# Pairing the key halves for the attention maxima: one 1024-column reduction, and seven PSUM banks shared out anew

## The reference

```python
xs = jnp.reshape(x, (B, T, C))                       # B 16, T 1024, C 128, x is layer-normed
scores = jnp.einsum('bhtd,bhsd->bhts', q, k) * scale # q, k: 8 heads x 1024 x 16
att = jax.nn.softmax(scores, axis=-1)                # needs the maximum over all 1024 keys
out = jnp.einsum('bhts,bhsd->bhtd', att, v)
...
x = x + _L0_conv_ref(_ln_c(x), ...)
t = _to_tokens(x)
t = t + _L0_ffn_ref(_ln_t(t), w_gating, w1, w2)      # top-2 gating over 16 experts
```

## Time and profile before

| | us |
|---|---|
| median of 3 runs | 2329.85 |
| lowest, highest | 2327.37, 2330.93 |
| span of the profiled execution | 2326.0 |
| TensorE busy (records overlap the drain) | 2117.5 (91%) |
| VectorE busy | 1840.5 (79%) |
| ScalarE busy | 1544.5 (66%) |

### The profile page before, as it was taken

One profiled execution on the slowest core, in us unless ns is written; L12 is line 12 of the kernel. 1 busy time (PEld: TensorE's weight loads), 2 busy tenths in 40 slices (PEclk: granted clock), 3 DMA queues, 4 the chain that ended last, 5 costly groups with the idle time before them and its releaser, 6 DMA issues. The chain is left out here.

```text
span 2326.0 us, 48689 instructions
## 1 busy us (share of the span) xinstructions
PE 2117.5 (91%) x14610; PEld 1160.1 (50%) x14610; DVE 1840.5 (79%) x4370; ACT 1544.5 (66%) x3153; POOL 1046.1 (45%) x1650
## 2 busy tenths in 40 slices
PE   6989999998999999999989999999888999999996
PEld 3333333333333333333333333333328999999996
DVE  6899989899899989899898999999954544445564
ACT  1677777777776777767676767777664666556553
POOL 3203444443434444444534445444344577645442
PEclk9999999999999999999999999999998999999997
DMA  4222223231323233231323332232233222222576
GB/s 123 47 41 57 57 56 69 42 71 35 68 47 65 49 67 61 49 74 35 68 39 64 55 63 58 56 59 43 61 118 112 72 71 82 89 65 70 155 241 184
DMA packets 135676, 170.79 MB, mean 73 GB/s; under 512 B 31568, under 2 KB 101592, under 8 KB 135414
## 3 DMA queue, kind: packets, MB, share of 16 engines
q1 hardware_dynamic: 118582, 134.25, 26.7%
q0 software_dynamic: 16896, 34.12, 4.2%
HBM read 64.86 MB, written 48.87 MB: 49 GB/s over the span
## 5 line engine op out<-in xcount | busy, mean ns | idle before, releaser
L978 DVE TENSOR_REDUCE sb_m_red<-banks 128x1 f32<-128x512 f32 x2048 | 1326.4, 678 | 154.6 <-PE banks L1491 153.1
L818 ACT ACTIVATE sb_arena_a<-banks 128x512 f32<-128x512 f32 x2048 | 1114.7, 599 | 444.3 <-PE banks L1515 421.2
L1491 PE MATMUL banks<-sb_arena_b 62*128 62x512 f32 x2048 | 815.2, 468 | 104.6 <-DVE sb_m_red L978 91.8
L1515 PE MATMUL banks<-sb_arena_b 64*128 64x512 f32 x2048 | 807.6, 463 | 7.1 <-ACT sb_arena_a L818 7.0
L1491 PEld LDWEIGHTS banks<-sb_arena_b 62*128 62x128 f32 x2048 | 347.6, 188 | 770.7 <-DVE sb_m_red L978 658.1
L1532 PE MATMUL banks<-sb_arena_a,sb_arena_d 128*32 128x512 f32 x4096 | 552.2, 611 | 6.5 <-ACT sb_arena_a L818 0.7
L747 POOL DMA_INDIRECT sorted_rows<-sb_rows,sb_place x256 | 251.4, 982 | 349.0 <-PE banks L1515 318.1
L791 POOL DMA_INDIRECT expert_out<-sb_arena_d x272 | 272.0, 1000 | 240.1 <-DVE sb_arena_d L1368 178.1
L1515 PEld LDWEIGHTS banks<-sb_arena_b 64*128 64x128 f32 x2048 | 338.4, 186 | 28.4 <-ACT sb_arena_a L818 28.0
L1657 PE MATMUL banks<-sb_arena_d,sb_arena_c 128*128 128x128 f32 x2176 | 290.8, 277 | 0.5 <-DVE sb_arena_c L1358 0.5
L1666 PE MATMUL banks<-sb_arena_c 128*128 128x128 f32 x2176 | 288.3, 276 | 0.0
(11 more groups left out here) (166 smaller groups left out, 1620.1 us busy)
## 6 DMA issues: line engine op xcount, KB each, us to landing
sb_arena_b<-sb_arena_c SPq DMA_DIRECT2D x768, 64.0 KB, 2.3
sb_arena_d<-sorted_rows SPq DMA_DIRECT2D x272, 66.0 KB
sb_x_in<-in_x_dram SPq DMA_DIRECT2D x16, 512.0 KB, 3.5
sb_res<-in_x_dram SPq DMA_DIRECT2D x16, 512.0 KB, 3.2
sb_x_all<-sb_res SPq DMA_DIRECT2D x16, 512.0 KB, 3.1
expert_out<-sb_arena_d POOLq DMA_INDIRECT x272
sorted_rows<-sb_rows,sb_place POOLq DMA_INDIRECT x256
sb_arena_a<-in_L_ffn_w_dram SPq DMA_DIRECT2D x4, 1024.0 KB, 7.1
```

Source lines behind the costliest of these rows:

```text
L818: nc.scalar.activation(probs[:, u % PRING, :], ps_score[:, u % RING, :], ACT.Exp, scale=SCALE).then_inc(exp_done, 1)
L978: nc.vector.tensor_reduce(out=m_red[:, s % 2, at:at + 1], in_=ps_max[:, m % SLOTS % RING, :], axis=AX.X, op=ALU.max).then_inc(max_taken, 1)
L1491: nc.tensor.matmul(ps_max[:, m % SLOTS % RING, :], qs[rows_of, g, l, half * HALF + t * P:half * HALF + (t + 1) * P], ks[rows_of, g, l, kh ...
L1515: nc.tensor.matmul(ps_score[:, u % RING, :], ks[rows_of, g, l, i * P:(i + 1) * P], qs[rows_of, g, l, half * HALF:(half + 1) * HALF], start ...
```

## The change

The two key halves of the same 128 queries and head now stand in neighbouring units: unit m even is keys 0 to 511, m odd keys 512 to 1023, and `side` changes every two units. They go to neighbouring banks of a ring of four (banks 3 to 6), and VectorE takes both with one maximum of 1024 columns, negated, straight into `m_neg`; `row_maxima` and `m_red` are gone. `LEAD` is 44, the order of a step's four heads is 1, 3, 0, 2 (`HEAD_AT`), so that M and S keep to opposite rows. The two steps of `split_m` come one step earlier. `ps_pv` is bank 7. There is no `misc` bank: scores and all other products go round the banks 0 to 2 in the order in which TensorE issues them (`front_order`), each waiting for the reader of the product three before it. `choose` starts at step 36 instead of 38.

```diff
-LEAD = 45
+LEAD = 44
+HEAD_AT = (1, 3, 0, 2)
 MSLOT = 24
-RING = 3
+FRONT, MRING = 3, 4
...
+FRONT_BANK = {what: n % FRONT for n, what in enumerate(front_order())}
...
-        ps_score, ps_max = banks[:, 0:RING], banks[:, RING:2 * RING]
-        ps_pv, misc = banks[:, 6], banks[:, 7]
+        ps_max, ps_pv = banks[:, FRONT:FRONT + MRING], banks[:, FRONT + MRING]
+        def front(what, b, i=0):
+            return banks[:, 4] if b == B - 1 and what in LATE else banks[:, FRONT_BANK[what, b, i]]
...
-                nc.vector.tensor_reduce(out=m_red[:, s % 2, at:at + 1], in_=ps_max[:, m % SLOTS % RING, :], axis=AX.X,
-                                        op=ALU.max).then_inc(max_taken, 1)
-
-            def row_maxima(b, s):
-                k = STAGES * b + s
-                wait(dve, max_taken, UNITS * (k + 1))
-                wait(dve, m_split, 2 * (k - 1))
-                nc.vector.tensor_reduce(out=m_neg[:, s % 2, :],
-                                        in_=m_red[:, s % 2, :].rearrange("p (n s) -> p n s", s=2),
-                                        axis=AX.X, op=ALU.max, negate=True).then_inc(m_ready, 1)
+                if u == 1:
+                    wait(dve, m_split, 2 * (STAGES * b + s - 1))
+                nc.vector.tensor_reduce(out=m_neg[:, s % 2, u // 2:u // 2 + 1],
+                                        in_=ps_max[:, m % MRING - 1:m % MRING + 1, :].rearrange("p k t -> p (k t)"),
+                                        axis=AX.X, op=ALU.max, negate=True).then_inc(max_taken, 1)
...
-                    if not (last and m >= SLOTS):
+                    if m % 2 and not (last and m >= SLOTS):
                         take_max(b, m)
...
+            def take(bank, sem_, value):
+                if freed[bank] is not None:
+                    wait(pe, *freed[bank])
+                freed[bank] = (sem_, value)
...
-                side, kh, t, l = u % SIDES, u // SIDES % 2, u // (2 * SIDES) % 4, u // (8 * SIDES)
+                kh, side, t, l = u % 2, u // 2 % SIDES, u // (2 * SIDES) % 4, u // (8 * SIDES)
...
-                wait(pe, max_taken, SLOTS * b + ring_free(m))
-                nc.tensor.matmul(ps_max[:, m % SLOTS % RING, :],
+                if kh == 0:
+                    wait(pe, max_taken, (SLOTS * b + m - MRING) // 2 + 1)
+                nc.tensor.matmul(ps_max[:, m % MRING, :],
...
-                wait(pe, exp_done, SLOTS * b + ring_free(u))
+                to = take_front("score", b, u, exp_done, SLOTS * b + u + 1)
```

More of the change, by code:

```diff
@@ L93, in wait_apart, with front_order @@
         eng.sem_inc(passed, 1)
-def ring_free(n):
-    return n - RING + 1 if n % SLOTS >= SLOTS % RING else n - SLOTS % RING + 1
+XT_AT, QK_AT, V_AT = (1, 5), (33, 41, 44, 48), (51, 54)
+OUT_AT, TOK_AT, LOGITS_AT, COUNT_AT = (13, 17), (20, 22), 36, 77
+assert SLOTS % MRING == 0
+def front_order():
+    yield from (("xt", 0, 0), ("xt", 0, 1), ("wg", 0, 0))
+    yield from (("qk", 0, i) for i in range(4))
+    yield from (("v", 0, 0), ("v", 0, 1), ("m", 0, 0))
+    for b in range(B):
+        for u in range(SLOTS):
+            yield "score", b, u
+            if b < B - 1:
+                yield from (("xt", b + 1, i) for i, at in enumerate(XT_AT) if at == u)
+                yield from (("qk", b + 1, i) for i, at in enumerate(QK_AT) if at == u)
+                yield from (("v", b + 1, i) for i, at in enumerate(V_AT) if at == u)
+            if b > 0:
+                yield from (("out", b - 1, i) for i, at in enumerate(OUT_AT) if at == u)
+                yield from (("tok", b - 1, i) for i, at in enumerate(TOK_AT) if at == u)
+                if u == LOGITS_AT:
+                    yield "logits", b - 1, 0
+                if u == COUNT_AT:
+                    yield "counts", b - 1, 0
+            if u % UNITS == MSLOT and not (b == B - 1 and u > 96):
+                yield ("m", b, u // UNITS + 1) if u // UNITS + 1 < STAGES else ("m", b + 1, 0)
+LATE = ("out", "tok", "logits", "counts")
+FRONT_BANK = {what: n % FRONT for n, what in enumerate(front_order())}
 def norms_before(b, s):
@@ L994, in split_m @@
                 if step == 0:
-                    wait(dve, m_ready, k + 1)
+                    wait(dve, max_taken, UNITS // 2 * (k + 1))
                     wait(dve, m_psum, k)
@@ L1451, in _, with take_front @@
         def _(pe):
-            freed = [None]
-            def misc_free(sem_, value):
-                if freed[0] is not None:
-                    pe.wait_ge(*freed[0])
-                freed[0] = (sem_, value)
+            freed = [None] * 8
+            def take(bank, sem_, value):
+                if freed[bank] is not None:
+                    wait(pe, *freed[bank])
+                freed[bank] = (sem_, value)
+            def take_front(what, b, i, sem_, value):
+                take(4 if b == B - 1 and what in LATE else FRONT_BANK[what, b, i], sem_, value)
+                return front(what, b, i)
             def transpose_x(b, half):
-                misc_free(xt_copied, 2 * b + half + 1)
+                to = take_front("xt", b, half, xt_copied, 2 * b + half + 1)
                 wait(pe, x_loaded, 16 * (b + 1))
                 for j in range(4):
-                    last = nc.tensor.transpose(misc[:, j * P:(j + 1) * P],
+                    last = nc.tensor.transpose(to[:, j * P:(j + 1) * P],
                                                x_in[:, (4 * half + j) * P:(4 * half + j + 1) * P], ident[:, :])
@@ L1590, in batch @@
             def batch(b, first, last):
-                freed[0] = (m_copied, STAGES * b + 1)
                 for u in range(SLOTS):
@@ L1688, in transpose_y @@
                     last.then_inc(yt_psum, 1)
-            pe.wait_ge(m_copied, STAGES * B)
+            for bank in range(FRONT):
+                wait(pe, *freed[bank])
             transpose_block(0, 0)
```

131 lines of the change are left out of this document (56 added, 75 removed).

## The result

| | before | after |
|---|---|---|
| median, us | 2328.61 | 2454.82 |
| lowest, highest of 4 runs | 2326.43, 2330.93 | 2453.53, 2456.2 |
| span of the profiled execution | 2326.0 | 2453.0 |

The ratio is 1.0549, 95% interval 1.0534 to 1.0565: slower by 126 us, where 2452 was predicted. The first score starts at 62.9 us (before 64.4) and the last at 1860.8 (before 1735.8). So the attention's steady part is 126.5 us longer; the start gains 1.5, and the tail, the experts' phase, is 2.0 longer.

A forecast was written before the change was run, and what follows sets the result against it. A loop through TensorE and VectorE was taken as the bound, closed by W inside a pair. Base 104.2 plus additions 9.2 gave 113.4 us a batch against 105.5, over 15.66 batches 124 us more: 2452 us, range 2370 to 2500 (75%).

The forecast's parts named there:

- quiet cycle: Four attention steps with only M, S, W, maxima and exponentials: 3.25 us after the change, against 2.72 now.
- two cycles with divisions, steps 2 to 10: In a stage's eighth cycle W comes behind the odd M, but VectorE's divisions make that cycle 3.3 us.
- both v projections and m, two cycles: v projections at steps 51 and 54, where S(54) and m wait for copies: 9.75 us, 3.2 more than two cycles.
- choice and norm means: Choice of experts and norm means, where VectorE's work comes near 3.25 us: 0.5 us added per batch.
- The loop: W inside a pair: maximum to even M 1.28, to W 0.43, to odd M 1.00, to its maximum 0.54; 3.25 us.
- D: Time on VectorE from one 1024-column maximum to the next: 1.15 us, with 1.05 and 1.24 as alternatives.
- The additions: Other products and waits on top of the base of 104.2 us a batch: 9.2 us in sum.
- Rival 1: VectorE is freed and its share of idle time stays: time 2205 to 2240 us; chance 5%.
- Rival 2: The loop holds but nearly all additions find cover: 0 to 3 us more a batch, 2325 to 2370 us; chance 12%.
- Rival 3: TensorE idles more and its clock falls, or more waits come in the shared ring: over 2500 us; chance 8%.
- the two terms downward, 44 and 72: Possible errors over the attention: 1024-column maxima 1.05 us apart, 44 us less; half of the additions hidden, 72 us less.
- three candidates for the quiet part: Before the change, four quiet steps: loop through TensorE and VectorE 2.72 us, VectorE alone 2.48, TensorE alone 2.45.

The follow-up runs named there:

- the better slots: Changed kernel with other products and their copies moved to other steps: 2266.27 us with every weighing W behind the odd M, 2442.47 us with W back inside the pair.
- the first experiment: Changed kernel with every weighing W one step later, behind the odd M of a pair, nothing else: 2388.38 us, ratio 1.0272 to the kernel before.
- the fastest kernel: Changed kernel with every weighing W behind the odd M and the other products and their copies moved to other steps: 2266.27 us, ratio 0.9738 to the kernel before.

## Why the prediction was right, and where it was not

| term | predicted | measured in after |
|---|---|---|
| quiet cycle | 3.25 | 3.23 to 3.25 |
| start of the 1024 maximum to the even M | 1.28 | 1.28 |
| odd M to its maximum | 0.54 | 0.53 |
| two cycles with divisions, steps 2 to 10 | 6.55 | 6.71 |
| two cycles with output projections | 7.3 | 7.49 |
| second tokens and m | 4.60 | 4.53 |
| q or k at 33; at 44 and 48 | 3.61 each | 3.70; 3.42 and 3.44 |
| logits and k at 41, two cycles | 8.5 | 8.34, and 9.13 with W at half clock |
| both v projections and m, two cycles | 9.75 | 9.66 |
| choice and norm means | 0.5 | nearly 0 away from the divisions |
| a batch | 113.4 | 113.3 |

- **The loop** was right in each of its four steps. The maximum takes 1216 ns, and of two back to back (2.35 together, from 849.38) the second starts 1.14 after the first, so D is 1.14 for 1.15: the slope over the columns held. The 0.62 for an old maximum was 2.48 / 4 and holds a quarter of the last one's tail; their starts are 0.60 apart and the release is 0.15, with the same sum of 0.75.
- **Where W stands** is the cause. In the better slots one line of the program is worth 176 us (2442 against 2266). In the original slots the same line gives 66, with waits at the shared banks in the way, and the pairs moved under W give 110 (1.0549 against 1.0076), there together with the order of heads and the choice's steps.
- **The remaining 18 us** weren't taken apart. Sharing the banks cost as much with single maxima in a ring of three (1.008), but with as many banks as the change has, four, single maxima stood at before's time (1.0005, 2327 us) and joined ones at 2343 (1.0076). So in the original slots the joined maximum is, if anything, 16 us slower than single ones, part of which may be the eighth W that is left inside a pair. Only in the better slots does it gain.
- **The additions** were right in sum by some luck: the outputs cost 0.2 more than I gave them together, the divisions 0.2 more at each of their four places, the q and k products at 44 and 48 0.2 less each, the choice some 0.4 less. Over a batch some 1.3 us too little stand against 1.1 too much. A step of the working is missing: a product in the scores' ring waits 0.2 for an exponential before it starts (0.24 at 33). I counted only waits of scores for copies.
- **Rival 1** (VectorE freed) fell: VectorE's idle time before maxima nearly doubled. **Rival 2** was right that additions can find cover, but not under this loop. **Rival 3** stayed small: clock 1.00 in the window, 3 W in 13 batches at the lower level, some 0.8 us each.
- The Trainium skill, "VectorE: DVE Perf Modes" (section on the TRN2 errata), gave the estimate of 128 us saved by one large maximum in place of two. The maxima's work fell by 92 us where both forms ran in the same slots, so the direction agrees and the size is 0.72 of the estimate; the time fell by 11 there, and in the original slots it didn't fall.
- **The range:** its lower end of 2370 takes the two terms downward, 44 and 72, as not coming together; both would give 2336. Nothing turned on it.
- **Wrong afterwards:** the expectations of the first experiment took TensorE's 2.45 as the floor behind the loop. The prediction's three candidates for the quiet part (maxima's loop, VectorE, TensorE) lacked a fourth, the scores' ring through ScalarE at 2.64. It lay under before's 2.71 and after's 3.24, so the prediction didn't need it; each statement on what comes next did.

## What to carry to other kernels

Joining two work items into one instruction on the consumer makes the producer's two halves one item too: whatever the producer does between them is added to the buffer's loop once a cycle, and if a long product stands there, that can cost more than the consumer saves, as it did here (3.24 us a cycle in place of 2.71). Before a resource that looks short is relieved, write down every closed loop through each ring of buffers (here M's through VectorE, S's through ScalarE) with its hand-overs; the longest one is the cycle, and the second longest limits what can be gained. A buffer shared by several kinds of products makes the slowest reader everyone's wait, so product and reader must be placed together.

## What the runs showed of the hardware that I had not expected

- A VectorE product of 128x8 with both inputs in SBUF took 1.81 to 2.02 us in place of 0.17 when it fell into a GpSimd addition of 128x1024 (2.35 us), and moving it gained 44 us in one kernel and 41 in another. A lead of 45 in place of 44 made the two meet in one (0.17 to 2.02), a fourth bank in another (0.38 to 1.81).
- Behind a wait of TensorE of 1.7 us (on the logits' reader) or 2.3 us (on that product) W ran at the lower level (granted clock 0.50) in those traces, 1.93 in place of 1.07. But it did so too where TensorE's records show no gap, behind the 16-column logits, in 3 of 13 batches of after, and for all or part of a W in 7 of 15 of the fastest kernel. What tells these batches from the others stays open.
- In the first maxima (20 to 60 us) the mean granted clock was 0.63 in after and 1.00 in before, and yet the first score came 1.5 us earlier.
